# Bias table stored in the second image step, padding rows behind the level rows, filler products at other waits of a vision tower kernel

## The reference

```python
def tokens(x):                      # three levels, patch sizes 1, 2, 4
    for idx, W, b, p in levels:     # idx: Hilbert order of the patches
        t = patches(x, p)[:, idx].reshape(B, -1, 16 * p * p * 3)
        outs.append(t @ W.T + b)    # 256, 64 and 16 tokens of 64
    y = concat([outs[0], interp(outs[1], 256), interp(outs[2], 256)])
    return y @ Wf.T + bf            # [16, 256, 192]

def attention(x):                   # 12 heads of 16, T = 256
    q, k, v = split(x @ w_qkv)
    y = softmax(q @ k.T / 4) @ v @ w_out + b_out
    return layernorm(y) * ln_g + ln_b

def ffn(x):                         # 16 experts, top 2 of 16
    gate = top2(softmax(x @ Wr.T))
    for e in range(16):
        y += gate[e] * (gelu(x @ W1[e] + b1[e]) @ W2[e] + b2[e])
    return x + y

h = tokens(x)
h = h + attention(layernorm(h))
h = h + ffn(layernorm(h))
```

## Time and profile before

| what | us |
|---|---|
| three runs | 814.27, 810.04, 808.65 |
| median of them | 810.04 |
| span of the profiled execution, first to last instruction | 776.9 |
| median less span | 33.1 |
| TensorE's matmuls busy in the span | 693.9 |
| mean granted clock of TensorE | 0.969 |

### The profile page before, as it was taken

How to read it: one execution, slowest core, us unless ns; L and a number is a source line. 1 busy time by engine, 2 the same in 40 slices (tenths; PEclk the granted TensorE clock), 3 DMA queues, 4 the chain that set the end, 5 groups by cost and what they waited for, 6 DMA issues and landing times.

```text
span 776.9 us, 22765 instructions
## 1 busy us (share of the span) xinstructions
PE 693.9 (89%) x7879; PEld 598.0 (77%) x7879; DVE 459.1 (59%) x1322; ACT 372.5 (48%) x892; POOL 389.3 (50%) x599
## 2 busy tenths in 40 slices
PE   0597689999999999999889999999999999999970
PEld 0486557777677777777657999999999999999970
DVE  7301345788888888888876764444444444443448
ACT  0232246666666666666565433334434453443443
POOL 6772123557777777777666553333433343343320
PEclk9999769999999999999999999999999999999995
DMA  8776624434444444444429634748348325498159
GB/s 208 140 114 190 140 60 108 112 89 121 103 110 103 111 115 114 109 109 111 108 66 264 189 106 121 220 141 227 91 128 236 97 76 149 123 288 240 50 182 331
DMA packets 96795, 110.69 MB, mean 142 GB/s; under 512 B 18625, under 2 KB 85186, under 8 KB 96386
## 3 DMA queue, kind: packets, MB, share of 16 engines
q1 hardware_dynamic: 79202, 79.56, 39.6%
q0 software_dynamic: 11792, 27.18, 11.7%
q10 hardware_dynamic: 5712, 2.79, 2.0%
HBM read 142.13 MB, written 33.96 MB: 227 GB/s over the span
## 4 chain that ended last, share of the span: by engine, by line
PE 57%; DVE 12%; issue 9%; POOL 8%; DMA 5%; SPq 4%; ACT 1%; POOLq 1%; DVEq 0%; ACTq 0%
PE BK L506 20%; PE BK L494 20%; PE BK L828 4%; PE BK L962 3%; PE BK L921 2%; POOL slot_rows L1896 2%; POOL rs L1845 2%; PE BK L941 2%; DVE negmax L1567 2%; DMA level_patches<-pixels 2%; POOL hr L1885 1%; DVE hr L694 1%; PE BK L973 1%; DMA level_rows<-shared 1%; SPq L746 1%
## 5 line engine op out<-in xcount | busy, mean ns | idle before, releaser
L530 ACT ACTIVATE pixels<-BK,shared 128x128 f32<-128x128 f32 x474 | 130.7, 375 | 197.1 <-PE BK L494 166.0
L494 PE MATMUL BK<-pixels,shared 64*128 64x128 f32 x2844 | 172.8, 272 | 2.0 <-issue 2.0
L506 PE MATMUL BK<-shared,pixels 64*128 64x192 f32 x1896 | 172.4, 328 | 2.3 <-DVE pixels L670 2.2
L704 POOL DMA_INDIRECT pair_rows<-pixels x79 | 77.9, 985 | 190.4 <-DVE pixels L670 183.9
L494 PEld LDWEIGHTS BK<-pixels,shared 64*128 64x128 f32 x2844 | 169.1, 188 | 3.3 <-issue 3.1
L506 PEld LDWEIGHTS BK<-shared,pixels 64*128 64x128 f32 x1896 | 153.3, 188 | 4.3 <-issue 3.9
L1567 DVE TENSOR_REDUCE negmax<-BK 128x6 f32<-128x1536 f32 x64 | 112.4, 1757 | 27.9 <-PE BK L941 26.6
L1317 ACT ACTIVATE shared<-BK 128x1536 f32<-128x1536 f32 x64 | 92.7, 1448 | 9.5 <-PE BK L962 9.1
L1896 POOL DMA_INDIRECT slot_rows<-xr,adr x64 | 64.7, 1011 | 36.8 <-issue 13.8
L669 DVE TENSOR_TENSOR pixels<-BK,shared 128x192 f32<-128x192 f32 x79 | 28.2, 357 | 71.1 <-PE BK L506 70.8
L656 DVE TENSOR_TENSOR pixels<-pixels 128x1 int32<-128x1 f32 x64 | 10.2, 159 | 89.9 <-PE BK L480 89.9
(11 more groups left out here) (239 smaller groups left out, 1073.6 us busy)
## 6 DMA issues: line engine op xcount, KB each, us to landing
shared<-ew SPq DMA_DIRECT2D x158, 288.0 KB
shared<-ew SPq DMA_DIRECT2D x79, 576.0 KB
shared<-qk_parts SPq DMA_DIRECT2D x112, 96.0 KB
shared<-expert_biases SPq DMA_DIRECT2D x79, 99.0 KB
pixels<-slot_rows POOLq DMA_DIRECT2D x64, 104.0 KB
qk_parts<-shared SPq DMA_DIRECT2D x32, 192.0 KB, 2.0
shared<-qk_parts SPq DMA_DIRECT2D x16, 288.0 KB
shared<-pair_rows SPq DMA_DIRECT2D x12, 384.0 KB, 7.6
```

Of the source, the lines that this page charges most:

```text
L494: last = nc.tensor.matmul(hidden(t)[h * HC + c], w1h[w][rows, (k + h) % NK, c * P:(c + 1) * P], xtT[p][rows, k, :], start=(c == 0 and k == ...
L506: last = nc.tensor.matmul(Y[h], hT[p][rows, c * P:(c + 1) * P], w2b[w][rows, c, :], start=(c == 0), stop=(c == FC - 1))
L530: last = nc.scalar.activation(hT[p][:, c * P:(c + 1) * P], hidden(t)[c], ACT.Gelu, bias=bias[w][:, c:c + 1])
L704: nc.gpsimd.indirect_dma_start(pair_d, bass.IndirectOffsetOnAxis(t_dst[:, t:t + 1], 0), ysum[t % NB][:, :], None).then_inc(s[f"m_sc{t % NB ...
```

## The change

It has four edits.
- ACT's two DMAs of the bias table leave `copies` and are issued at the end of ACT's image step 1 (`store_biases`), with the same wait before them.
- POOL waits for the level-2 rows in `hrow` (`ld_o2`) before it issues the stores of the padding rows.
- 5 units leave step -3, and 6 units are issued at the end of `level1`, behind the wait for the level-1 rows and ahead of the waits for `dve_wf` and the level-2 rows.
- Step -1 gets 10 units ahead of the first scores of image 0, and 3 ahead of its third group of scores.

```diff
             def level1():
...
                 pe.wait_ge(s["act_o1"], B // 2)
+                keep(6)
                 pe.wait_ge(s["dve_wf"], 2)
                 pe.wait_ge(s["ld_o2"], 16)
...
                 if on(0):
                     a_st(i, p, 0)
+                filling(at1=10)
                 if on(1):
                     a_s(i + 1, q, 0)
...
-                filling(at3=5, at2=2)
+                filling(at2=2)
                 if on(3):
                     pe.wait_ge(s["act_xs"], i + 4)
...
                 if on(3):
                     f_h(i + 3)
-                filling(at3=9, at2=8)
+                filling(at3=9, at2=8, at1=3)
                 if on(1):
                     a_s(i + 1, q, 2)
...
-                act.wait_ge(s["act_wf"], 2)
-                nc.scalar.dma_start(bias_d[:, :, 0:FC].rearrange("e p c -> p e c"), b1T[:, :, :]).then_inc(s["st_bias"], 16)
-                nc.scalar.dma_start(bias_d[:, :, FC:FC + E], eb2.unsqueeze(1).to_broadcast([NE, P, E])) \
-                    .then_inc(s["st_bias"], 16)
                 act.wait_ge(s["pe_x1T_"], 1)
...
+            def store_biases():
+                act.wait_ge(s["act_wf"], 2)
+                nc.scalar.dma_start(bias_d[:, :, 0:FC].rearrange("e p c -> p e c"), b1T[:, :, :]).then_inc(s["st_bias"], 16)
+                nc.scalar.dma_start(bias_d[:, :, FC:FC + E], eb2.unsqueeze(1).to_broadcast([NE, P, E])) \
+                    .then_inc(s["st_bias"], 16)
...
                 if on(0):
                     a_oT(i, 1)
                     a_oT(i, 2)
+                if isinstance(i, int) and i == 1:
+                    store_biases()
...
             pool.wait_ge(s["dve_init"], 4)
+            pool.wait_ge(s["ld_o2"], 16)
             nc.gpsimd.dma_start(slot_d[0:NE * SEG, :].rearrange("(e s) c -> e s c", e=NE)[:, 0:P, :]
```

More of the change, by code:

```diff
@@ L875, in level2, with keep @@
                 last.then_inc(s["pe_o2"], 1)
+            def keep(n):
+                for _ in range(n):
+                    nc.tensor.matmul(ST[:, 0, 0:E], ident[:, :], lng_b[:, :], start=True, stop=True)
             def level1():
@@ L886, in level1 @@
                 pe.wait_ge(s["act_o1"], B // 2)
+                keep(6)
                 pe.wait_ge(s["dve_wf"], 2)
                 pe.wait_ge(s["ld_o2"], 16)
-            def keep(n):
-                for _ in range(n):
-                    nc.tensor.matmul(ST[:, 0, 0:E], ident[:, :], lng_b[:, :], start=True, stop=True)
             def f_xT(n):
```

## The result

The changed kernel takes 820.01 us (median of 4 runs, 816.41 to 824.46) against 809.35 for the kernel before beside it: ratio 1.0133, 95% interval 1.0087 to 1.0178. It is 1.3% slower; the forecast of 811.8 had the direction (1.75 us slower) but was 8.2 us short, and 820.0 lies above its range (800 to 818). Two later measurements, on two chips, gave 1.0107 and 1.0109.

What follows compares the result with a forecast made beforehand. TensorE, busy 89% of the span, was taken as the bound, with lower-clock stretches after waits. Terms -3.0 - 6.0 + 0.8 + 0.95 + 7.0 + 2.0 = +1.75 gave span 778.7, time 811.8; range 800 to 818.

Steps and rivals of the forecast that it cites:

- The base: Whole kernel: profiled span 776.9 us, median 810.04; the 33.1 us between them was kept as a constant distance.
- -8.2 for the front: Everything ahead of image step 2: -3.0 at level rows and first projection, -6.0 and +0.8 in step -1.
- Taken: -3.0: Level rows, filler, first projection: first transposes 2.5 us earlier, about 0.5 more from the clock; bounds -2.5 to -3.5.
- -6.0: Wait at 88.66, first image's q and k: filler holds the clock, saving 3.9 to the transposes, 2.1 behind them.
- +0.8: Open 2.52 us wait before 104.04: half of the 1.65 us a lower clock there would cost.
- the new wait of POOL on the level rows: Start, before the padding stores: costs nothing, as the level rows land before POOL's last gather at 61.72.
- +0.95: End of ACT's image step 1: the two table issues delay ACT's next instruction without cover; 0.5 to 1.5.
- +7.0: Image step 2: SP's store of image 2's transposed maxima is served behind the table, so TensorE waits; from 0 if queues share.
- +2.0: Image step 2, behind that wait: one short stretch of lower clock; 0 to 3.3.
- The first rival: Image step 2: queues share, so no wait; sum -7.25, time 802.8 (799 to 806); chance 0.30.
- The second: Image step 2, from second-half scores on: clock stays low, some 10 us in place of 2.0; 819.8; chance 0.08.
- The third: Step -1: filler does not hold the clock, so no 6.0 and 0.8; sum +6.95, time 817.0; chance 0.12.

Runs made afterwards that it cites:

- the filler alone: Kernel before with all filler units placed as in the changed kernel, store and POOL untouched: 808.49 us, ratio 0.9966.
- the kernel before once more: Kernel before, unedited, measured and profiled a second time: 813.42 us, ratio 1.0009, profile span 809.6.
- the store alone: Kernel before with only the bias-table stores moved to the end of ACT's image step 1: 824.44 us, ratio 1.0133.
- the last kernel: Kernel before with the filler moved and the table stored by SP in three parts, no POOL wait on the level rows: 775.47 us, ratio 0.9941.
- the units of step -1 alone: Kernel before with only the 10 units ahead of image 0's first scores and 3 ahead of the third group: 775.29 us, ratio 0.9933.
- the changed kernel with the store back: Changed kernel with ACT's two bias-table stores back in the start, the rest kept: 811.99 us, ratio 0.9997.
- the parts alone: Kernel before with the table stored by SP in three parts behind the second-half maxima of images 0 to 2: 810.04 us, ratio 0.9978.
- the store back, second time: Changed kernel with ACT's bias-table stores back in the start, measured again on another chip: ratio 0.9963.

## Why the prediction was wrong

**The base.** "The median is 810.04, 33.1 us above it, and I keep that distance." This is the step that failed first, and with it the front's terms. In the changed kernel's profile the execution took 818.64 us with a span of 816.9, so 1.7 us lie around a span; some 30 of the 33.1 were inside the timed executions, as a wait that the profile did not show. A time 33 us above its span was the sign of it, and it was in the table ahead of the prediction. The forecast's -8.2 for the front came out as some -2.2.

**"Taken: -3.0" for level rows and first projection.** In the one profile of the kernel before with the start-up wait there is nothing to gain. From the start of level 1 to the first scores it takes 36.64 us (79.69 to 116.33), the changed kernel 36.59, 36.73 and 36.17 in three profiles; in the first profile it was 40.25. The pixels are there because the gathers have long ended. The level rows are in time for another reason: the table took as long as before (15.0 us against 15.9), but the products between its issue and level 1 ran slowly, so that level 1 began 10.5 us behind the issue in place of 6.6. Where they ran at full pace, in the filler alone, the store of the level rows took 10.2 us, behind the table again, and the rows landed at 88.2; TensorE stood 0.26 us behind its 6 units, and without them would have stood 2.3 (an estimate: 88.2 less 85.9, where the units start). So with the start-up wait this term lies between 0 and some 2 us, by the execution. Where the wait is missing the mechanism is there: the first transposes start at 62.5 with the units moved and 61.6 with the table away as well, against 64.39, so -1.9 and -2.8.

**"-6.0" and "+0.8" for the wait at 88.66.** The mechanism held to a tenth: 11.9 us from the load to the transposes forecast, 11.95 measured in nine of eleven profiles with the ten units (13.63 in two, where the clock fell in between). The size was wrong, for two reasons. The cover to be gained is smaller with the start-up wait: 13.8 to 14.75 without the units in place of 15.4. And the clock falls at the open 2.52 us after all. Measured from first scores to step 1's q projection, the stretch of both effects: 34.1 us in the mean of the four profiles with the start-up wait and without the units (32.4 to 36.3), 32.8 in the nine with them (32.06 to 33.96), so -1.3; without the start-up wait 36.0 in three and 32.8 in two, so -3.2. The 0.8 charged for the open wait was half of what came in each of the eleven: that projection took 3.1 us in the mean (2.44 to 3.62) in place of 1.89, and the scores beside it 1.22 in place of 0.83 in the changed kernel, together some 1.6.

**"So the new wait of POOL on the level rows costs nothing [...] and the padding rows start when they did."** In the timed executions the second half does not hold: POOL stood 23.9 us for the level rows in the changed kernel and issued the padding stores at 80.41, against 56.50 in the kernel before once more. The price is open: 1.0038 alone, where the start-up wait is missing (0.9997 to 1.0079), and none seen with it.

**"+0.95", "+7.0", "+2.0" for step 2.** Right in kind and place, and somewhat small. From the transposed maxima of image 2's second half to those of image 3 the kernel before takes 18.51 us (165.54 to 184.05), the changed kernel 29.36, 31.07 and 30.39, the store alone 29.74: 10.9 to 12.6 more, where the sum had 9.95. In the changed kernel 1.70 are ACT's hold (the second issue took 1.74), 0.28 and 6.81 the waits on SP's queue, and the rest, 10.85 - 1.70 - 7.09 = 2.1, is put down to the lower clock. The timed price is 9.9 to 12.0.

**Together:** -2.2 + 11 = +8.8 us on 810, where I had +1.75; some 6 of the missing 7 are the front's, measured against a profile that was not of the executions timed. The first rival (queues that share) is refuted by the packets: 1545 of ACT's and none of SP's in 8 us, and 1635 to 5 in the store alone (173 to 181 us). The second (a clock that stays low) has 819.8, all but the measured 820.01, but for a cause that did not come: the granted clock was 0.61 for 7 us and then 1.00, where that rival needed over 12 us at the lower level. The third, with 817.0, is wrong in its reason: the filler does hold the clock at the first scores.

**What stays open:** what the change does where the start-up wait is missing. The terms measured there for the front (0.9953 and 0.9933, POOL's wait 1.0038: -3.7, -5.2 and +3.0 us) and the 10 to 12 us of the store would leave it 4 to 6 us slower if they add, and some 8 to 10 if the units together give only the 4.6 of the last kernel (0.9941). Both are estimates. What holds the engines while the gathers run, and why one chip does not show it, is open too.

## What to carry to other kernels

Set a profile's span beside the times before building a sum on it: if they differ by more than the two or three us around a span here (1.7 to 2.8 in the profiled executions), the profile is of another course of events, and terms taken from its waits may not exist. In these runs a large DMA delayed what was issued behind it in its transfer time, on its own queue and on the other: look for the first small store that something waits for, and put the large one right behind that, in pieces shorter than the gap to the next. Filler pays where it stands in the wait itself, and the next open wait takes part of it back.

## What the runs showed of the hardware

While POOL issues indirect gathers, one each 1.25 us, other engines can stand for no reason that the trace names: 30 us at one place, or product by product with 1.6 to 2.3 us between. The four chips of the other runs showed this in every profile, and all their times are above 800 us; one chip showed it in no profile, with all times below 790; what differs on that one is open. The hold ends 4 to 8 us after the last gather (64.2 against 56.5, 81.3 against 77.1).

A granted clock of 1.00 is no proof of full rate: level 2's 24 products took 4.17 us in some profiles and up to 6.9 in others, of the same kernel too. It came without the start-up wait as well (6.67 in the units of step -1 alone). Neither the table nor the padding rows decide it: it took 4.17 with the table in the start (the changed kernel with the store back) and 6.80 without it (the parts alone), 6.93 with POOL's wait (the store back, second time) and 4.17 without (the filler alone). The stretch of the kernel before once more, with products of 6.81 us in it (length, PE busy, clock, DMA share, GB/s):

```profile
66.00:79.00 13.00, 12.95 (x68) 1.00 0.85 186
```

Together with the transposes ahead of it (4.8 to 6.4 us) that makes some 4 us of spread between executions ahead of the image loop: from ACT's copy of `w2f` to level 1 the kernel before once more took 15.5 us and the changed kernel 11.3.

Issuing the table's large DMA from ACT took 1.73 to 2.38 us in the image loop (four profiles) and 0.97 to 1.38 in the start, but 2.52 there in the filler alone.
